# A recommendation tower on one core: one-hot columns in quarters, other banks and joins at the end, and a new order behind the second selection

## The reference

```python
e = jnp.stack([tbl_f[ids[:, f]] for f in range(26)], axis=1)       # 2048 x 26 x 128
combined = jnp.concatenate([dense[:, None, :], e], axis=1)          # 2048 x 27 x 128
inter = jnp.einsum('bfd,bgd->bfg', combined, combined)
z = jnp.concatenate([dense, inter[:, iu, ju]], axis=1)              # 351 pairs
h = jnp.concatenate([z, dense], axis=1)                             # 607 columns
h = jnp.maximum(h @ W_top1 + b_top1, 0.0)                           # 607 x 512
h = jnp.maximum(h @ W_top2 + b_top2, 0.0)                           # 512 x 256
y = h @ W_top3                                                      # 256 x 1
```

## Time and profile before

| | us |
|---|---|
| three runs, median (lowest to highest) | 451.1 (450.58 to 453.02) |
| the profiled execution | 452.48 |
| its span | 450.7 |
| PE busy, with 3496 matmuls | 413.7 |
| VectorE busy | 312.7 |
| ScalarE busy | 255.1 |
| GpSimd busy | 236.2 |

### The profile page before, as it was taken

The page is one execution under the profiler, slowest core; times in us unless marked ns, Lnnn a source line. Parts: engine busy times, 40 slices in busy tenths (PEclk is TensorE's granted clock), DMA queues, the critical chain, the costliest instruction groups (busy, mean ns, idle before and its releaser), DMA issues.

```text
span 450.7 us, 9538 instructions
## 1 busy us (share of the span) xinstructions
PE 413.7 (92%) x3496; PEld 392.5 (87%) x3496; DVE 312.7 (69%) x970; ACT 255.1 (57%) x577; POOL 236.2 (52%) x247
## 2 busy tenths in 40 slices
PE   0867799989999999999999899999999999998997
PEld 1756699979998899989998799988999799988976
DVE  4898498786777857776777857777777876744351
ACT  3785667383455745375454844466452945459462
POOL 5677355555655566655566456555565556653000
PEclk9999699999999999999999999999999999999999
DMA  6999514232233172322522153221533243111000
GB/s 183 251 237 263 123 50 93 73 62 63 85 75 81 40 98 62 78 65 61 86 67 80 44 85 70 76 78 43 100 71 67 64 70 73 42 42 31 1 2 0
DMA packets 25407, 36.47 MB, mean 81 GB/s; under 512 B 6197, under 2 KB 19645, under 8 KB 25362
## 3 DMA queue, kind: packets, MB, share of 16 engines
q1 hardware_dynamic: 17682, 20.13, 21.7%
q0 software_dynamic: 7680, 15.74, 13.8%
HBM read 35.84 MB, written 0.01 MB: 80 GB/s over the span
## 4 chain that ended last, share of the span: by engine, by line
PE 75%; DVE 7%; issue 5%; DMA 4%; ACT 4%; SPq 3%; DVEq 0%; ACTq 0%
PE gram_ps L481 22%; PE x_ps L463 16%; PE x_ps L464 15%; PE tail_ps L521 5%; DVE hot L942 5%; PE tail_ps L522 5%; PE tail_ps L523 4%; PE x_ps L443 4%; DMA raws<-in_tbl_dram 4%; PE tail_ps L514 2%; SPq L349 2%; ACT x L695 2%; DVE pairs L926 1%; DVE gram L926 1%; ACT pairs L695 1%
## 5 line engine op out<-in xcount | busy, mean ns | idle before, releaser
L410 POOL DMA_INDIRECT rows<-in_tbl_dram,ids_sb x240 | 235.4, 981 | 178.7 <-PE x_ps L463 63.5
L942 DVE TENSOR_SCALAR hot<-ids_all,row_f 125x256 fp32r<-125x256 int32 x636 | 193.0, 373 | 51.8 <-PE x_ps L464 29.3
L463 PE MATMUL x_ps<-hot,table_hi 125*128 125x256 f32 x656 | 169.3, 294 | 23.4 <-DVE table_lo L929 10.2
L464 PE MATMUL x_ps<-hot,table_lo 125*128 125x256 f32 x656 | 164.0, 285 | 0.0
L463 PEld LDWEIGHTS x_ps<-hot,table_hi 125*128 125x128 f32 x656 | 126.2, 192 | 29.6 <-issue 20.0
L464 PEld LDWEIGHTS x_ps<-hot,table_lo 125*128 125x128 f32 x656 | 126.5, 193 | 0.0
L481 PE MATMUL gram_ps<-x 128*108 128x108 f32 x1024 | 108.3, 259 | 0.9 <-issue 0.9
L481 PEld LDWEIGHTS gram_ps<-x 128*108 128x108 f32 x1024 | 102.9, 175 | 2.0 <-ACT x L695 0.7
L695 ACT ACTIVATE picked<-x_ps 128x256 f32<-128x256 f32 x88 | 33.6, 382 | 97.7 <-PE x_ps L464 75.6
L695 ACT ACTIVATE gram<-gram_ps 44x208 f32<-44x208 f32 (+3 forms) x136 | 46.0, 338 | 29.1 <-PE gram_ps L481 24.3
L926 DVE COPY gram<-gram_ps 44x208 f32<-44x208 f32 (+1 forms) x120 | 44.3, 369 | 13.1 <-PE gram_ps L481 9.3
(11 more groups left out here) (82 smaller groups left out, 414.8 us busy)
## 6 DMA issues: line engine op xcount, KB each, us to landing
ids_all<-in_selected_ids_dram SPq DMA_DIRECT2D x83, 128.0 KB
raws<-in_tbl_dram SPq DMA_DIRECT2D x11, 448.0 KB
rows<-in_tbl_dram,ids_sb POOLq DMA_INDIRECT x240
rows<-in_r_dense_features_dram SPq DMA_DIRECT2D x16, 64.0 KB
stage<-in_W_pairs_dram SPq DMA_DIRECT2D x1, 702.0 KB
ids_start<-in_selected_ids_dram SPq DMA_DIRECT2D x5, 128.0 KB
raws<-in_tbl_dram SPq DMA_DIRECT2D x11, 52.0 KB
stage<-in_W_dense_dram SPq DMA_DIRECT2D x2, 256.0 KB
```

What stands on the lines that cost most here:

```text
L410: pool.indirect_dma_start(out=rows[t][:, slot, :], out_offset=None, in_=tables[GATHERED[slot - 1]], in_offset=bass.IndirectOffsetOnAxis(ap ...
L463: first = pe.matmul(bank, table_hi[j][:, c, :], v, start=(c == 0), stop=False)
L464: last = pe.matmul(bank, table_lo[j][:, c, :], v, start=False, stop=(c == VC - 1))
L942: last = dve.tensor_scalar(hot_buffers[hot_place(number)][:, c, :], ids, row, None, ALU.is_equal)
```

## The change

- The one-hot columns come in four buffers of two chunks (ten in the start) of the same size in all. PE tells of each quarter that it has read, and waits for each quarter. ScalarE's builds in the start write their second half in two steps.
- `picked` is split; the part for the second tile `t = 1` and tables 0 to 5 is double. `join(m, 1, 0)` moves behind `pick(m, 3)`, and `join(m, 0, 1)` from the end of the tile before to behind `pick(m, 0)` (except for the first and the last macro tile).
- In the last macro tile the two joins of its second tile are VectorE's. Layer 1's dense products are taken out of `layer1` and issued earlier, into the banks of the gram products.
- On PE, `select(m, 2)` follows `select(m, 1)`; `pair_transposes` 2 stands behind it, then a gram product, then `pair_transposes` 3. On VectorE, build 2 follows build 1, and the copies of pairs 1 and 3 stand behind it.

```diff
@@ -48,8 +48,9 @@
     EVEN = VK // 16 * 16
     TABLE_PARTS = (slice(0, EVEN), slice(EVEN, VK))
-    HALF = VC // 2
-    HOTS = 2
+    HOTS = 4
+    QUARTER = VC // HOTS
     IDS = 6
     assert IDS < NS <= 2 * IDS
...
@@ -95,16 +96,17 @@
-    START_HOTS = 5
-    ACT_HOTS = [2 * j + 1 for j in range(1, NS, 2)]
+    START_HOTS = 10
     def hot_number(m, j, h):
-        return m * 2 * NS + 2 * j + h
+        return (m * NS + j) * HOTS + h
+    ACT_HOTS = [hot_number(0, j, h) for j in range(1, NS, 2) for h in range(HOTS // 2, HOTS)]
     def hot_place(number):
-        return number % START_HOTS if number < 2 * NS else number % HOTS
+        return number % START_HOTS if number < HOTS * NS else number % HOTS
     def hot_ahead(number):
...
-    LAST_BANKS = [2, 3, 2, 3, 0, 2, 3, 1, 0, 2, 3, 1, 0, 2]
+    LAST_BANKS = [2, 3, 2, 3, 0, 2, 3, 4, 5, 6, 7, 1, 0, 2]
...
-        picked = sb("picked", [D, NS, MACRO])
+        picked_a = sb("picked_a", [D, 1 + 2, IDS, P])
+        picked_b = sb("picked_b", [D, NS - IDS, MACRO])
...
-        hot = [sb(f"hot{i}", [VK, HALF, MACRO], F32R) for i in range(HOTS)]
+        hot = [sb(f"hot{i}", [VK, QUARTER, MACRO], F32R) for i in range(HOTS)]
...
         tail_banks = tail_ps + [b[:].rearrange("p a b -> p (a b)") for b in x_ps]
+        tail_banks += [b[:, i, :] for b in gram_ps for i in range(UNIT_BANKS)]
...
-        tail_moved = [sem(f"tail_moved{i}") for i in range(4)]
+        tail_moved = [sem(f"tail_moved{i}") for i in range(4 + N1)]
...
+        def joined_slots(t, part):
+            j0, j1 = part * IDS, min((part + 1) * IDS, NS)
+            return x_slots(t, 1 + NG + j0, 1 + NG + j1).rearrange("d b f -> d f b")
+        def picked_rows(m, t, part):
+            if part == 1:
+                return picked_b[:, :, t * P:(t + 1) * P]
+            return picked_a[:, 0 if t == 0 else 1 + m % 2, :, :]
         def ids_of(m, j):
...
-            m, j, h = number // (2 * NS), number // 2 % NS, number % 2
-            if h == 0:
-                eng.wait_ge(hot_read, m * NS + j + 1)
+            m, j, h = number // HOTS // NS, number // HOTS % NS, number % HOTS
+            if h < HOTS - 1:
+                eng.wait_ge(hot_read, (HOTS - 1) * (m * NS + j) + h + 1)
             elif m == 0:
                 eng.wait_ge(x_filled, x_before(0, start_use(j) + 1))
...
                 bank = bank[:].rearrange("p a b -> p (a b)")[:, 0:MACRO]
                 for c in range(VC):
-                    number = hot_number(m + 1, j, c // HALF)
-                    if c % HALF == 0:
+                    number = hot_number(m + 1, j, c // QUARTER)
+                    if c % QUARTER == 0:
                         pe.wait_ge(*hot_done(number))
-                    v = hot_buffers[hot_place(number)][:, c % HALF, :]
+                    v = hot_buffers[hot_place(number)][:, c % QUARTER, :]
                     first = pe.matmul(bank, table_hi[j][:, c, :], v, start=(c == 0), stop=False)
                     last = pe.matmul(bank, table_lo[j][:, c, :], v, start=False, stop=(c == VC - 1))
                     if c % 2 == 1:
                         first.then_inc(paced, 1)
-                    if c == HALF - 1:
+                    if c % QUARTER == QUARTER - 1 and c < VC - 1:
                         last.then_inc(hot_read, 1)
...
-            def layer1(m, n):
+            def layer1_dense(m, n):
+                if is_last(m):
+                    pe.wait_ge(gram_moved[n // UNIT_BANKS], (m + 1) * UNITS)
                 bank = tail_bank(m, Q_H1 + n)[:, 0:MACRO]
                 cols = slice(n * P, (n + 1) * P)
                 pe.wait_ge(dense_kept, m + 1)
                 add_product(bank, [w[:, cols] for w in w1d], [v[:].rearrange("p s g -> p (s g)") for v in dense_t],
                             start=True).then_inc(paced, 1)
+            def layer1(m, n):
+                if not is_last(m):
+                    layer1_dense(m, n)
+                bank = tail_banks[tail_at(m, Q_H1 + n)[0]][:, 0:MACRO]
+                cols = slice(n * P, (n + 1) * P)
                 for c in range(KC):
                     wait_tail_moved(pe, m, Q_CHUNK + c)
                     k = slice(0, KP + (c == 0))
...
                 select(m, 1)
+                select(m, 2)
                 if before:
                     pair_transposes(m - 1, 2)
+                gram_products(m, 0, 0)
+                if before:
                     pair_transposes(m - 1, 3)
-                select(m, 2)
-                if before:
                     chunk_transposes(m - 1, 0)
                     chunk_transposes(m - 1, 1)
-                gram_products(m, 0, 0)
                 transposes(m, 1, 0)
                 if before:
...
@@ -639,11 +666,15 @@
                 layer1(m - 1, 3)
                 gram_products(m, 1, 3)
                 layer2(m - 1, 0)
+                layer1_dense(m, 0)
+                layer1_dense(m, 1)
                 pair_transposes(m, 0)
                 pair_transposes(m, 1)
                 layer2(m - 1, 1)
                 pair_transposes(m, 2)
                 pair_transposes(m, 3)
+                layer1_dense(m, 2)
+                layer1_dense(m, 3)
                 layer3(m - 1)
...
             def pick(m, j):
-                if isinstance(m, int) and m < 0:
+                if j % IDS == 0:
+                    wait(act, joined[0], 2 * m + j // IDS + 1)
+                    wait(act, joined[1], 2 * m + 2 * (j // IDS))
+                into = m + 1
+                if m < 0:
                     m, k = 0, start_use(j)
                 else:
-                    if j % IDS == 0:
-                        act.wait_ge(joined[1], 2 * m + j // IDS + 1)
                     k = x_use(m, "table", j)
                 bank = x_bank_of(m, k)
                 act.wait_ge(x_filled, x_before(m, k + 1))
                 src = x_ps[bank][:].rearrange("p a b -> p (a b)")[:, 0:MACRO]
-                copy(picked[:, j, :], src).then_inc(x_moved[bank], 1)
+                if j < IDS:
+                    second = 1 + into % 2
+                    src = src.rearrange("p (t b) -> p t b", t=TILES)
+                    copy(picked_a[:, 0:second + 1:second, j, :], src).then_inc(x_moved[bank], 1)
+                else:
...
-                j0, j1 = part * IDS, min((part + 1) * IDS, NS)
+                j1 = min((part + 1) * IDS, NS)
                 wait(act, gram_filled, (m - 1) * (TILES * UNITS) + (t + 1) * UNITS)
                 if t == 0:
                     k = start_use(j1 - 1) if m == 0 else x_use(m - 1, "table", j1 - 1)
                     for i in range(2):
                         act.wait_ge(x_moved[i], x_before(max(m - 1, 0), k + 1, i))
-                copy(x_slots(t, 1 + NG + j0, 1 + NG + j1).rearrange("d b f -> d f b"),
-                     picked[:, j0:j1, t * P:(t + 1) * P]).then_inc(joined[t], 1)
+                copy(joined_slots(t, part), picked_rows(m, t, part)).then_inc(joined[t], 1)
             def keep_dense(m):
...
             def macro_tile(m, before):
                 transposes(m, 0, 2)
-                join(m, 1, 0)
                 pick(m, 0)
+                if m > 0:
+                    join(m, 0, 1)
                 if before:
                     pair_transposes(m - 1, 0)
                 transposes(m, 0, 3)
                 pick(m, 1)
+                pick(m, 2)
                 if before:
                     pair_transposes(m - 1, 2)
-                pick(m, 2)
                 if not before:
                     split_w1p()
                 if before:
...
                     layer1(m - 1, 0)
                 pick(m, 3)
+                join(m, 1, 0)
                 if not before:
                     split_w2()
...
                 pick(m, 10)
                 transposes(m + 1, 0, 0)
-                join(m + 1, 0, 1)
+                if is_last(m + 1):
+                    join(m + 1, 0, 1)
                 transposes(m + 1, 0, 1)
                 if before:
                     layer3(m - 1)
...
                 transposes(m, 0, 3)
                 pair_transposes(m - 1, 0)
-                join(m, 1, 0)
                 pair_transposes(m - 1, 2)
...
                 chunk_transposes(m - 1, 0)
                 chunk_transposes(m - 1, 1)
-                join(m, 1, 1)
                 gram_products(m, 0, 2)
                 chunk_transposes(m - 1, 2)
...
-                wait_hot_read(act, hot_ahead(number))
-                act.wait_ge(distances_ready, ACT_HOTS.index(number) + 1)
-                act.activation(hot_buffers[hot_place(number)], distance, ACT.Relu, bias=1.0,
-                               scale=-1.0).then_inc(act_hot_ready, 1)
+                act.wait_ge(distances_ready, built + 1)
+                for i in range(2):
+                    number = hot_number(0, j, HOTS // 2 + i)
+                    wait_hot_read(act, hot_ahead(number))
+                    act.activation(hot_buffers[hot_place(number)], distance[:, i * QUARTER:(i + 1) * QUARTER, :],
```

(18 more changed lines are left out.)

23 lines of the change are left out of this document (12 added, 11 removed).

## The result

| | median, us | lowest to highest | span of the profiled execution |
|---|---|---|---|
| before | 451.08 | 450.58 to 453.02 | 450.7 |
| after | 468.56 | 467.57 to 470.81 | 467.0 |

The changed kernel is slower: 1.0386 times the time before, with a 95% interval of 1.0338 to 1.0434. The forecast was 457.1 with a range of 453.0 to 461.0. Its sign is right, and the time lies 7.6 us above the range. Every ratio and interval in this document leaves out the slow runs, those over 1.5% above the fastest of their kernel (one of e1's four and two of before's 23 in the second group of experiments), while the medians count them.

The account below looks back on a forecast made before the run. PE was taken as the bound, with about one microsecond idle per steady tile. Steady tiles +9.1, start and first tile -2.3, last tile -0.8 sum to +6.0 on 451.1: 457.1 us, range 453 to 461.

Parts of the forecast that it names:

- S0: `select(m, 0)`, a macro tile's first selection: would start 2.80 us behind the tile's start in place of 3.21, 0.4 gained.
- S2: `select(m, 2)`, a macro tile's third selection: would start at 9.32 us against 9.80, 0.5 gained in all.
- The chain behind S2: Steady tiles: pair transposes 3 behind a gram product delay build 3; chunk transposes 2 at 16.86 against 15.23, 1.63 us later.
- Start: Start and first tile: quartered columns shorten the last start step and waits for build 2 and later; together -2.3 us.
- its first part: End of the start: four matmuls remain in place of eight on the ScalarE chain to the first selection, 0.5 us gained.
- Last tile: Last macro tile: joins moved to VectorE cost 0, early dense products of layer 1 gain 1.4 - 0.6, so -0.8 us.
- Rival D, the signals: Selections: the quarters' added PE signals each cost a fifth of a matmul, 3.6 us together; kernel at 461, chance 0.04.
- Rival C, the clock: Transposes and idling before the gram product behind `pair_transposes` 3 lower the clock; 460 to 463, or 475 us; chance 0.10.
- the sum +9.1 - 2.3 - 0.8: Whole kernel: steady tiles +9.1, start and first tile -2.3, last tile -0.8, giving +6.0 us.
- one of 4.6 us that had fallen and one of 3.2 that had not: Kernel before: transposes only in the start, clock then 0.50; transposes with layer 3 at a steady tile's start, no fall.

Follow-up runs that it names:

- e1: Kernel before with the new order behind the second selection on PE and VectorE, ScalarE left as it was; 476.97 us.
- e4: Changed kernel with `pair_transposes` 3 moved ahead of the gram product on PE; 452.84 us.
- e8: Kernel before with only layer 1's dense products of the last tile issued early, in four banks of their own; 451.58 us.
- e2: Changed kernel with the old order behind the second selection on PE and VectorE, ScalarE left in the new order; 468.47 us.
- e3: Changed kernel with 16 filler gram products on PE in the wait ahead of chunk transposes 2; 469.37 us.
- e12: Kernel before with the one-hot columns in quarters and nothing else; 445.67 us.
- e5: Changed kernel with 8 filler gram products on PE in the wait ahead of chunk transposes 2; 460.37 us.
- e11: Changed kernel with the 8 filler gram products in the first steady tile alone; 464.54 us.
- e7: Changed kernel with the whole old order behind the second selection, on PE, VectorE and ScalarE; 449.58 us.

## Why the prediction was right in its sign and wrong in its size

**S0 and S2: right.** S0 has no wait and stands 2.65 behind the tile's start (forecast 2.80), the third selection at 9.30 (forecast 9.32), behind ScalarE's chain of pick, join, pair copies and copy, as forecast. (The chain's terms as written, 4.98, 0.3, 1.2, 2.0 and 0.7, add up to 9.18 and not to 9.26; nothing hangs on it.)

**The chain behind S2: right.** Chunk transposes 2 came at 16.95 in the tile shown and at 16.3 to 16.95 in all (forecast 16.86), the idle time before them was 1.67 (forecast 1.8), VectorE waited 2.67 before the copies of pairs 3 (forecast over 2), and the low part of `pairs_t` is the releaser. The one steady tile that kept its clock took 53.15 (forecast 53.3). Six tiles gave +9.1 for the forecast's +9.1. e4 shows that it is this one transpose behind the gram product: with it ahead, the wait shrinks to 0.1 to 0.4.

**Start: right in its sum alone.** The forecast was -2.3 and the trace shows -2.4, but its first part failed: S0 of the first tile starts at 50.15 against 50.07, behind the same 1.11 us of wait for ScalarE, so the quarters gained nothing there in place of 0.5. What made up for it was the clock, which is luck: low for 3.4 us in the first tile of after, for 6.8 in before. In e4, whose clock was low there for 6.8 as in before, the gain is 1.6. One execution alone doesn't bear more than this: e8, whose start is before's, had no low clock there and reached its second tile at 89.42, 1.3 earlier than before.

**Last tile: about right.** It is 0.5 longer, with one fall of the clock in it. e2 and e3 have the same last tile without a fall, and it took 48.8 and 48.7: the fall cost 1.5, and the rest is -0.9 to -1.0. e8 measures the dense products by themselves at -0.96; the forecast was -0.8. VectorE's joins took 0.92 and 0.93 us each and PE waited for neither.

**Rival D, the signals: refuted.** e12 has all of the quarters' additional signals, 154 of them in the seven tiles with selections, and its steady tiles are 0.7 us shorter. From chunk transposes 2 to the next tile's start, a stretch with eight selections and 16 of these signals, PE takes 36.52 us in e12 and 36.50 to 36.57 in before. The Trainium skill ("TensorE: Matmul & The Clock Gate", "The cost: per-tile semaphore tail") gives about 26 ns for each, for small matmuls packed into one array, which would be an estimate of 4 us for the kernel; this case doesn't agree, and its added signals come four matmuls apart.

**Rival C, the clock: the step that failed.** The forecast had the mechanism and the place: transposes and idle time between the gram matmuls before `pair_transposes` 3 and the next gram product, 4.1 us. But the sum +9.1 - 2.3 - 0.8 has no term for the clock; the forecast gave it a chance of 0.10 and left all but its cheapest case out of the range, with the argument that the stretch stood between one of 4.6 us that had fallen and one of 3.2 that had not. That argument took the length for what decides. Two things were wrong with it. First, the range between two rows is unknown, not improbable; a stretch that repeats in six tiles and lies in the upper part of the gap belonged into the range. Second, the length alone doesn't decide: before's own stretch of 3.7 us in the last tile (409.22 to 412.92, above) kept its clock, the same instructions lost it in six other kernels, and e2 lost it behind 3.0 to 3.2 us, no longer than the row that was taken as safe. The price was off too, in the other direction: most falls took 3.4 us in place of 5 to 6 and cost 1.5 to 1.6, in place of 3. Five tiles with a fall, one of them twice as long, cost 9.1 us: 457.1 plus 9.1 plus 1.5 for the last tile is 467.7, against 468.6 measured. That this low clock comes from the stretch is shown by e5, which fills the wait and has no fall in the six tiles.
The Trainium skill (same page, Part 4: PE-mode transpose) has a transpose not counted as a matmul is. The traces are in line with it: PE waits 1.40 us before the third selection in after too, between matmuls, and no fall followed there in any tile, while one followed in six kernels behind the last tile's 3.7 us of transposes with only 1.2 us of waiting in them. No run replaced the transposes themselves by matmuls.

## What to carry to other kernels

A transpose whose result an in-order engine waits for belongs ahead of the matmuls that don't depend on it: here one transpose behind a gram product of 1.6 us cost 16 us in all, about half of it by the clock. When an edit leaves TensorE with transposes and waiting alone for some microseconds (here falls followed 3.0 to 4.8 us of it), price the low clock in every repetition, as a case of its own in the range, and don't take one execution without a fall as a reason against it. When a loss is found, undo the parts of a change one by one, on every engine that a part touches: the order was the whole loss, and the finer columns in the same change were worth 5.3 us.

## What was not expected of the hardware

The falls of after come about one tile apart: they begin at 105.52, 160.14, 214.75, 269.36 and 323.98, 54.6 us from each other every time, while the tiles there took 54.35 to 54.98. Between these falls the clock was up for 51.2 us each time, and no trace here has a fall in its tiles sooner than that behind the one before. It fits three of the stretches that escaped, which ended 49.5 to 50.0 us after the clock had come back: after's sixth steady tile (380.79, up since 330.80), e11's sixth, and e2's first. It doesn't explain the others, before's last tile and e11's second steady tile among them, where the clock had been up for longer. What sets whether such a stretch is followed by a fall is open; it was not tried to shift the tiles by a known delay alone. Nor is the kernel before free of it: one of its 23 executions beside e5 to e8, at 455.75 us, had a mean granted clock of 0.976, where the profiled one had 0.992.

`gram_products` issues eight matmuls per call (not 16, as the description of the kernel has it); they show as 16 instructions and take 1.6 us, so a matmul of this type counts as two. e3's doubled fillers came from overlooking it.

In e7, once, ScalarE began 2.7 us after the PE work that it waited for had ended by its record (139.25 against 141.98). VectorE, which waited for the same selection to free its columns, began at 141.98 too (in the rows of e7 above), so the delay was on PE's side, in its work or its signal, and not in ScalarE. Other executions of e7 took as little as 445.4 us, so it is probably not in all of them; its cause is open.
